# First feed-forward layer: rows centred by ScalarE, layer-norm steps and weight casts laid out anew

## The reference

```python
x = x + 0.5 * ffn(_layernorm(x), W_up, W_gate, W_down)
x = x + attention(_layernorm(x), Wq, Wk, Wv, Wo, head_scale)   # 16 heads, 4 key/value heads, rotary, causal
x = x + 0.5 * ffn(_layernorm(x), W_up, W_gate, W_down)

def ffn(x, ...):            # weights: clip(round(w / mean|w|), -1, 1) * mean|w|
    hidden = silu(x @ wu.T) * (x @ wg.T)      # 256 -> 1024
    return hidden @ wd.T                      # 1024 -> 256
```

## Time and profile before

| | |
|---|---|
| median of three runs | 1136.71 us |
| the profiled execution: its own time | 1136.0 us |
| its span (first to last instruction) | 1134.2 us |
| TensorE busy | 1073.0 us (95%) |
| VectorE busy | 959.3 us (85%) |
| ScalarE busy | 790.2 us (70%) |
| GpSimd busy | 719.0 us (63%) |
| first product of tile 0, of tile 1, last product of tile 7 | 20.43, 54.13, 224.44 us |

### The profile page before, as it was taken

One profiled execution on the slowest core, in us unless ns is written; L12 is line 12 of the kernel. 1 busy time (PEld: TensorE's weight loads), 2 busy tenths in 40 slices (PEclk: granted clock), 3 DMA queues, 4 the chain that ended last, 5 costly groups with the idle time before them and its releaser, 6 DMA issues.

```text
span 1134.2 us, 27100 instructions
## 1 busy us (share of the span) xinstructions
PE 1073.0 (95%) x8465; PEld 839.6 (74%) x8465; DVE 959.3 (85%) x2369; ACT 790.2 (70%) x1964; POOL 719.0 (63%) x886
## 2 busy tenths in 40 slices
PE   4697888979999999999999999999999998999998
PEld 2354555658888888888888888888888886555555
DVE  5787888699999999999999999999999997433433
ACT  4363665568878888878878788788787885554453
POOL 4653555567777777777777777777777773544443
PEclk9798999999999999999999999999999999999999
DMA  9421112134533443434344434334344344100101
GB/s 347 116 48 38 38 37 55 20 60 76 80 71 71 82 76 70 80 71 89 66 77 83 79 69 79 74 74 79 69 79 79 69 79 80 29 20 18 37 18 37
DMA packets 262130, 79.88 MB, mean 70 GB/s; under 512 B 249296, under 2 KB 260816, under 8 KB 261840
## 3 DMA queue, kind: packets, MB, share of 16 engines
q1 hardware_dynamic: 261664, 79.19, 33.8%
q10 hardware_dynamic: 432, 0.27, 0.1%
HBM read 12.85 MB, written 4.19 MB: 15 GB/s over the span
## 4 chain that ended last, share of the span: by engine, by line
PE 70%; issue 10%; POOL 8%; DVE 7%; ACT 3%; DMA 1%; DVEq 0%; POOLq 0%; ACTq 0%
PE bank L666 45%; PE bank L727 14%; POOL SCR L386 6%; PE bank L655 4%; PE bank L627 3%; PE bank L637 3%; DVE X L853 1%; DVE SCR L863 1%; ACT SCR L557 1%; DMA SCR<-ARENA 1%; ACT SCR L473 1%; DVE SCR L827 1%; DVE ARENA L1032 1%; ACT NHL L465 1%; POOL RSTD L373 1%
## 5 line engine op out<-in xcount | busy, mean ns | idle before, releaser
L414 POOL TENSOR_SCALAR SCR<-SCR,RI 128x128 f32<-128x128 f32 (+1 forms) x512 | 309.3, 604 | 44.0 <-DVE RI L1028 3.8
L399 POOL TENSOR_TENSOR SCR<-SCR 128x512 f32<-128x512 f32 x160 | 203.2, 1270 | 150.2 <-DVE SCR L993 148.9
L557 ACT ACTIVATE SCR<-bank,NM 128x128 f32<-128x128 f32 (+1 forms) x512 | 208.5, 419 | 125.4 <-DVE NM L1012 125.4
L386 POOL TENSOR_TENSOR SCR<-SCR 128x512 f16<-128x512 f32 x128 | 154.2, 1205 | 196.4 <-ACT SCR L479 196.2
L863 DVE SCALAR_TENSOR_TENSOR SCR<-SCR,CS,bank 128x512 f32<-128x512 f32 x128 | 95.3, 745 | 128.7 <-PE bank L637 90.4
L727 PE MATMUL bank<-SCR 128*128 128x128 f32 (+1 forms) x1024 | 193.2, 331 | 3.7 <-ACT SCR L557 3.7
L529 ACT COPY SCR<-bank 64x512 f32<-64x512 f32 x320 | 185.7, 580 | 13.8 <-PE bank L666 7.3
L1032 DVE TENSOR_TENSOR ARENA<-SCR,ARENA 128x768 f16<-128x768 f32 x128 | 187.8, 1467 | 4.3 <-ACT ARENA L564 3.4
L666 PE MATMUL bank<-WOH,ARENA 128*128 128x256 f16 x1024 | 188.5, 273 | 2.2 <-DVE ARENA L1023 1.3
L479 ACT CAST SCR<-SCR 128x512 f16<-128x512 f32 x128 | 79.1, 618 | 152.8 <-DVE SCR L863 102.9
L1012 DVE CUSTOM_DVE_ANT_0 bank<-bank,MASK,SCQ 128x128 f32<-128x128 f32 (+1 forms) x512 | 182.9, 417 | 0.8
(11 more groups left out here) (113 smaller groups left out, 1646.7 us busy)
## 6 DMA issues: line engine op xcount, KB each, us to landing
out<-X SPq DMA_DIRECT2D x7, 512.0 KB, 2.9
X<-in_x SPq DMA_DIRECT2D x1, 2560.0 KB, 10.4
ARENA<-in_wq SPq DMA_DIRECT2D x1, 2048.0 KB, 12.9
ARENA<-in_wo SPq DMA_DIRECT2D x1, 2048.0 KB, 18.1
SCR<-ARENA SPq DMA_TRANSPOSE x128, 3.6
X<-in_x SPq DMA_DIRECT2D x3, 512.0 KB, 9.6
X<-in_wu SPq DMA_DIRECT2D x1, 1024.0 KB, 6.8
X<-in_wg SPq DMA_DIRECT2D x1, 1024.0 KB, 9.0
```

The source lines that it names most:

```text
L386: gp.tensor_tensor(HL[:, f % 4, :], H32[:, f % 2, :], HH[:, f % 4, :], ALU.subtract).then_inc(s["hl_done"], 1)
L399: gp.tensor_tensor(dst, M1[:, m, :], M2[:, m, :], ALU.add).then_inc(add, 1)
L414: last = gp.tensor_scalar(EX[:, par, lo:hi], EX[:, par, lo:hi], RI[:, par, c:c + 1], PS, ALU.mult, ALU.mult)
L557: last = act.activation(EX[:, par, 384 * hh + lo:384 * hh + hi], SBK[hh][:, lo:hi], ACT.Exp, bias=NM[:, par, c:c + 1], scale=-1.0, accum_o ...
```

## The change

1. `center` for jobs 1 to 14 goes from VectorE to ScalarE: `norm_center` computes `RSTD * x + NB` in four activations (Identity, with scale and bias both read per row). VectorE makes the bias `NB = -mean * RSTD` in one small step (`norm_bias`). Jobs 0 and 15 stay on VectorE.
2. The steps of each job are placed by a table of pieces (`NORMS`). For tiles 1 to 6 the even job has statistics in piece 0, bias in 2, centring, high and low part all in 3; the odd job has statistics in 4, bias in 6, centring in 7, high and low part in piece 1 of the next tile.
3. The comparison of the ternary weights goes from GpSimd to VectorE, and the order of the quarters is changed.
4. The largest magnitudes are spread over pieces 9 to 29, the head scale over pieces 10 to 17, the scales are made at the end of tile 3 and the start of tile 4, and the casts run in tiles 4 to 7 (`CUT0 = 4`): ScalarE in pieces 2, 2, 5 and 6, VectorE in 2, 5, 6 and 7.
5. All eight tiles of the first layer are written out on every compute engine.
6. TensorE runs 20 matmuls of a constant before the first transposes and 8 after them (`keep_warm`), and sums the second weight matrix (`total(1)`) before the first up product.
7. In `down`, for both layers, the first half of a tile's first down product waits for only half of the residual steps, and the second half for all.

The DMA queues' own list is unchanged.

```diff
-        CUT0 = 3
+        CUT0 = 4
...
+        TERNARY = {-1: [(0, 0), (1, 0)], 0: [(0, 1), (1, 1), (0, 2)], 1: [(2, 0)], 2: [(2, 1), (1, 2)], 4: [(0, 3), (1, 3)],
+                   5: [(2, 2)], 7: [(2, 3)]}
+        ORDER = [q for f in TERNARY for q in TERNARY[f]]
+
+        MAXIMA = {9: [(1, 0)], 13: [(0, 1)], 15: [(0, 0)], 18: [(2, 0), (3, 0)], 20: [(0, 2)], 21: [(3, 3)], 22: [(0, 3), (3, 1)],
+                  29: [(3, 2)]}
...
+        norm_job(1, 1, -1, 1, 2, 3, 3)
+        for n in range(1, TILES):
+            at = FC * n
+            if n < TILES - 1:
+                norm_job(2 * n, n + 1, at, at + 2, at + 3, at + 3, at + 3)
+                norm_job(2 * n + 1, n - 1, at + 4, at + 6, at + 7, at + 9, at + 9)
+            else:
+                norm_job(2 * n, n - 1, at + 3, at + 5, at + 6, at + 6, at + 7)
...
+            def norm_center(q, tile):
+
+                act.wait_ge(ln_nb, q)
+                if q == 1:
+                    act.wait_ge(ln_t0, DC)
+                else:
+                    act.wait_ge(ln_lo, q - 1)
+                for s in range(SUB):
+                    act.activation(XN[:, s // 2, :, s % 2, :], X[:, tile * (SUB * D) + s * D:tile * (SUB * D) + (s + 1) * D].rearrange("p (c d) -> p c d", c=DC),
+                                   ACT.Identity, bias=NB[:, s:s + 1], scale=RSTD[:, s:s + 1]).then_inc(ln_xn, 1)
...
+                    high(layer, n, f)
                     if layer == 0:
+                        for q, tile in norms("center", n, f):
+                            norm_center(q, tile)
+                        for q, tile in norms("hi", n, f):
+                            norm_hi(q, *turned_ahead(q))
                         weights(n, f)
...
+                for i, piece in enumerate((2, 2, 5, 6)):
+                    if n >= CUT0 and f == piece:
+                        act.wait_ge(a_sc, 1)
...
+            def keep_warm(times):
+
+                for _ in range(times):
+                    pe.matmul(GB[1][:, 0:P], IDF[:, :], IDF[:, :], start=True, stop=True)
...
                 if f == 0:
-                    wait(pe, s["x_done"], SUB * n)
+                    wait(pe, s["x_done"], SUB * n - SUB // 2 if not isinstance(n, int) or n > 0 else 0)
...
                 for sub in range(SUB):
+                    if f == 0 and sub == SUB // 2:
+                        wait(pe, s["x_done"], SUB * n)
...
             pe.wait_ge(consts, 5)
+            keep_warm(20)
             first_turn()
             total(0)
+            keep_warm(8)
+            total(1)
             ffn(0, 0, False)
...
+            def norm_bias(q):
+
+                ve.wait_ge(ln_rs, q + 1)
+                ve.scalar_tensor_tensor(NB[:, :], MV[:, :, 0], -1.0, RSTD[:, :], ALU.mult, ALU.mult).then_inc(ln_nb, 1)
...
+                    if layer == 0:
+                        for q, _ in norms("lo", n, f):
+                            norm_lo(q)
                     if f == LAG - 1 and prev:
                         residual(layer, n - 1)
...
                     if layer == 0:
+                        for q, tile in norms("stats", n, f):
+                            if tile < n:
+                                ve.wait_ge(s["x_done"], SUB * tile + SUB)
+                            stats(q, tile)
+                        for q, _ in norms("bias", n, f):
+                            norm_bias(q)
                         weights(n, f)
...
+                for i, at in enumerate((2, 5, 6, 7)):
+                    if n >= CUT0 and f == at:
+                        raw, hi, lo, size, c = CUTS[i]
...
+                        ve.wait_ge(w_hi, (n - CUT0) * len(CUTS) + i + 1)
...
+            def ternary_piece(i, q):
+
+                raw, t = quarter(i, q)
+                ve.tensor_scalar(t, raw, FNEG[:, i:i + 1], None, ALU.is_lt).then_inc(less, 1)
+                ve.wait_ge(less, ORDER.index((i, q)) + 1)
+                ve.scalar_tensor_tensor(t, raw, FHALF[:, i:i + 1], t, ALU.is_gt, ALU.subtract).then_inc(tern[i], 1)
```

More of the change, by code:

```diff
@@ L373, in rstd, with ffn @@
                 gp.tensor_tensor(RSTD[:, :], VE[:, :], NEGHALF[:, :], ALU.pow).then_inc(ln_rs, 1)
-            def compare(f):
-                for i, q in LESS[f]:
-                    gp.wait_ge(f_sc, (1, 4, 6)[i])
-                    raw, t = quarter(i, q)
-                    gp.tensor_scalar(t, raw, FNEG[:, i:i + 1], None, ALU.is_lt).then_inc(less, 1)
-            def ffn(layer, n, jobs):
+            def ffn(layer, n):
                 s = ff[layer]
@@ L386, in ffn @@
                     gp.tensor_tensor(HL[:, f % 4, :], H32[:, f % 2, :], HH[:, f % 4, :], ALU.subtract).then_inc(s["hl_done"], 1)
-                    if layer == 0 and isinstance(n, int) and n == 0 and f in LESS:
-                        compare(f)
-                    for f0, _, _, q, _ in jobs:
-                        if f == f0:
+                    if layer == 0:
+                        for q, _ in norms("stats", n, f):
                             rstd(q)
@@ L465, in norm_hi, with high, ffn @@
                 act.copy(NHL[:, :, 0, :], rows.rearrange("p t c s d -> p t (c s d)")).then_inc(ln_hi, 1)
-            def ffn(layer, n, jobs):
+            def high(layer, n, f):
+                s = ff[layer]
+                j = FC * n + f
+                act.wait_ge(s["h_done"], j + 1)
+                wait(act, s["down_done"], j - 3)
+                act.copy(HH[:, f % 4, :], H32[:, f % 2, :]).then_inc(s["hh_done"], 1)
+            def ffn(layer, n):
                 s = ff[layer]
@@ L517, in _ @@
             act.wait_ge(f_sc, 1)
-            for n in range(CUT0):
-                ffn(0, n, ln_jobs(n))
-            with act.Fori(CUT0, TILES - 1) as n:
-                ffn(0, n, ln_jobs(n))
-            ffn(0, TILES - 1, ln_jobs(TILES - 1))
+            for n in range(TILES):
+                ffn(0, n)
             def rope_swap(r, m):
@@ L629, in up @@
                 last.then_inc(s["u_done"], 1)
-                if making and f == 0:
-                    total(1)
                 if making:
@@ new lines, in weights @@
+                piece = FC * n + f
+                for w, part in MAXIMA.get(piece, ()):
+                    ve.wait_ge(attn_raw, 64)
+                    if w == 3:
+                        ve.wait_ge(hs_mul, 4 * part + 4)
+                    ve.tensor_reduce(PMAX[:, 4 * part + w:4 * part + w + 1], (RQ, RK, RV, RO)[w][:, part * 1024:(part + 1) * 1024],
+                                     AX.X, ALU.max, apply_absolute_value=True).then_inc(a_part, 1)
+                if piece == max(MAXIMA):
+                    ve.wait_ge(a_part, 10)
+                    ve.wait_ge(ones, 2)
+                    ve.tensor_reduce(PM4[:, 0:4], PMAX[:, :].rearrange("p (j w) -> p w j", w=4), AX.X, ALU.max).then_inc(a_part, 1)
@@ L912, in ternary @@
             def ternary(f):
-                for i, q in TERNARY[f]:
-                    if f == -1:
+                if f == -1:
+                    for i in range(2):
                         ternary_scale(i)
-                    raw, t = quarter(i, q)
-                    if f == -1:
-                        ve.tensor_scalar(t, raw, FNEG[:, i:i + 1], None, ALU.is_lt).then_inc(tern_a, 1)
-                        ve.wait_ge(tern_a, i + 1)
-                    else:
-                        ve.wait_ge(less, LESS_ORDER.index((i, q)) + 1)
-                    ve.scalar_tensor_tensor(t, raw, FHALF[:, i:i + 1], t, ALU.is_gt, ALU.subtract).then_inc(tern[i], 1)
-                    if f == -1 and i == 0:
-                        first_lo()
+                        ternary_piece(i, 0)
+                        if i == 0:
+                            first_lo()
+                else:
+                    for i, q in TERNARY[f]:
+                        ternary_piece(i, q)
@@ L948, in ternary_scale, with diagonal @@
                     ve.wait_ge(f_sc, 7)
[L950 removed]
+            def diagonal():
                 ve.wait_ge(a_turn, 1)
```

140 lines of the change are left out of this document (45 added, 95 removed).

## The result

The changed kernel takes 1147.32 us (median of four runs, 1146.55 to 1148.32) against 1136.68 for the kernel before on the same chip: a ratio of 1.0093, interval 1.0076 to 1.0111. It is 10.6 us slower, and the forecast was 8.6. The profiled execution took 1146.98, its span is 1145.2, so the two profiles differ by 11.0.

| stretch | before | after | difference | forecast |
|---|---|---|---|---|
| start to first product of tile 1 | 54.13 | 43.51 | -10.62 | -10.3 |
| from there to the last product of tile 7 | 170.31 | 186.38 | +16.07 | +15.1 |
| last product to the query's rotary product | 4.19 | 11.42 | +7.23 | +5.9 |
| rotary product to first residual of the last stage | 758.94 | 759.42 | +0.48 | 0 |
| first to last residual of the last stage | 142.37 | 140.20 | -2.17 | -2.1 |

The account below looks back on a forecast made before the run. The chain silu, product, cast between ScalarE and VectorE was taken to set the pace. Last product 4.8 us later, passage 5.9 later, last stage 2.1 gained: 8.6 slower, 1145.3 us; own range 1140 to 1149, wider range 1134.5 to 1150.5.

Parts of the forecast that it names:

- The two lists: First-layer pieces: each takes the longer of ScalarE's 1.30 + extras + 0.72 and VectorE's 0.66 + extras; tile 5 27.25 us.
- The activation: ScalarE's centring: 0.50 us per activation to the next, 2.0 a job of four; low bound 1.6, high 2.12.
- The start: Up to tile 1's first product: first product at 18.1, tile 0 takes 25.7, tile 1 begins at 43.8; 10.3 us gained.
- Tile 7: Last tile of the first feed-forward layer: 22.3 us to its last product.
- The passage: First layer into attention: key projection waits for the last cast remainder, then matmuls are doubled; 5.9 us later, bounds 3.7 and 7.
- The last stage: Tile edges of the last stage: half the residual wait removes 0.3 us seven times; 2.1 us gained, bounds 0 and 2.3.
- both prices are at their low ends: Rival: centring activation 0.40 us and no clock drop in the passage; 1.1 us slower, 1137.8; chance 0.14.
- VectorE was the bound: Rival: ScalarE's idle time takes up centring, each job showing 1.0 instead of 2.0; 5.4 us faster, 1131.3; chance 0.13.
- the start gains less: Rival: tile 0's pieces are held up, so tile 1 begins at 48 instead of 43.8; 1149.5 us; chance 0.13.

Follow-up runs that it names:

- e3: The changed kernel with ScalarE's centring of jobs 1 to 14 as a multiplication by one per-row operand, mean not subtracted: 1142.27 us, ratio 1.0043.
- e9: The changed kernel with job 1's high and low part at pieces 5 and 6 of tile 0 instead of 3 and 3: 1151.72 us, ratio 1.0137.
- e1: The changed kernel with TensorE waiting for 14 of 16 casts before the key projection, all 16 before the first value projection: 1140.59 us, ratio 1.0031.
- e2: The changed kernel with the residual wait of the down product whole again, in both layers: 1150.64 us, ratio 1.0119.
- e10: The kernel before with centring of jobs 1 to 14 on ScalarE, bias step on VectorE, in the old pieces 1 and 5: 1165.17 us, ratio 1.0248.
- e5: The changed kernel with a new layout of pieces, centring on VectorE, key projection waiting for fewer casts: 1114.71 us, ratio 0.9812.

## Why the prediction was right, point by point

- **The two lists.** For tile 5 they gave 2.4, 3.5, 3.9, 5.6, then 2.4 for piece 5, 3.1, and 4.0 for piece 7; the trace has 2.26, 3.87, 3.76, 5.61, 2.39, 3.06 and 3.98. Tile 5's sum was to be 27.25 and is 27.18. Tiles 1 to 4 were forecast at 26.8, 29.3, 24.4 and 28.1, and took 27.05, 29.35, 24.54 and 27.64. The 3.87 is the piece that is furthest off: its low part took 1.60 instead of 1.22, for a reason that the last section shows. e3 is the test of the mechanism: 0.37 us less work behind the cast made each of these pieces 0.36 shorter.
- **The activation.** Taken at 0.50 to the next from the row with a per-row scale and the 0.1 of a second operand; measured 588 ns long, 0.50 to the next.
- **The start.** First product forecast 18.1, measured 16.91, and tile 0 25.7, measured 26.6: so the two errors cancel in 43.8 against 43.51, which is luck. The first half of a ternary quarter was priced at 0.83 from a row of the kernel before in which VectorE overlapped a GpSimd comparison; in tile 0 here it takes 0.48 (23.17, 26.06) or 1.38 (27.23, 34.84). e9 shows that it is job 1's place that pays.
- **Tile 7.** Forecast 22.3 to its last product, measured 23.44. The mis-sized pieces are 3 to 5, at 8.01 together for 6.8; e1 has them in 6.66 at a granted 1.00. This is TensorE at a lower granted clock, which the prediction had not counted there. In both kernels TensorE is idle 2.80 us ahead of these pieces; then a gate product takes 1.92 here, at a granted 0.50 (216 to 218), and 1.03 in e1. TensorE loses its lead by it and holds the next pieces to its own 2.60.
- **The passage.** The mechanism was right, the key projection behind the last cast remainder and then doubled matmuls; the size was 5.9, with 7 as its high bound, and 7.2 was measured, just outside. The term that failed most is the cast remainder's 1.37: WOL took 2.18. From the last product to the key projection I had 0.66 + 1.13 + 1.37 = 3.2, and it is 4.03. The query's projection is then 4.24 behind the key's, where 4.4 was forecast. The remaining 3.15 to the rotary product were forecast as 1.3 + 1.2 = 2.5: the query's first four matmuls still took 1.03, where the full clock makes it 0.60.
- **The last stage.** 0.31 less at each of seven edges, 2.17 in all, forecast 2.1. e2 gives it back.
- **The rivals.** That both prices are at their low ends fell with the row of 588 ns and the granted 0.50. By its own prices, 0.40 instead of 0.50 in 56 activations, that rival saves 5.6 and not 5.3, which changes nothing in the range. That VectorE was the bound fell with e10: the 13 jobs in tiles 1 to 7 cost 27.9 / 13 = 2.1 us each on average, more and not less (in tile 5 piece 1 is 2.9 longer and piece 5 1.5). That rival asked whether ScalarE's idle time takes up the centring; that idle time is ahead of the cast, and the centring is behind it. That the start gains less fell with 43.51.

## What to carry to other kernels

Where engines hand a chain round in order, write each step's list for each engine and take the longer; an extra behind the link of the chain costs its whole length, though the engine is busy only two thirds of the time, and an extra in the other engine's waiting time is free (piece 5 of tile 5 in e5 holds two cast remainders on VectorE and takes the 2.02 of a plain one). Choose the pieces and the engine together: here neither is good or bad alone, and one pair, with the short key wait, was 1.9% faster than the kernel before and another 2.5% slower. Let a wait cover only what the next instruction reads: two casts too many ahead of the key projection cost over 6 us.
